# Attention on Trainium2: the products by V issued four key chunks at a time in every fourth unit

## The reference, cut to what matters

```python
n_heads = 16
B, L, D = x.shape
head_dim = D // n_heads
qkv = (x @ Wqkv + bqkv).reshape(B, L, 3, n_heads, head_dim)
q, k, v = (qkv[:, :, 0], qkv[:, :, 1], qkv[:, :, 2])
scores = jnp.einsum('bqhd,bkhd->bhqk', q, k) / math.sqrt(head_dim)
...
scores = scores + slopes[None, :, None, None] * bias[None, None]
probs = jax.nn.softmax(scores, axis=-1)
out = jnp.einsum('bhqk,bkhd->bqhd', probs, v).reshape(B, L, D)
return out @ Wout + bout
```

## Time and profile before

| | us |
|---|---|
| median of 3 runs (3433.7 to 3438.01) | 3435.34 |
| the profiled execution | 3434.41 |
| its span, first to last instruction | 3432.8 |
| TensorE busy (92% of the span) | 3145.6 |
| VectorE busy (68%) | 2335.4 |
| ScalarE busy (53%) | 1823.5 |
| GpSimd busy (31%) | 1072.7 |

### The profile page before, as it was taken

How to read it: one execution, slowest core, us unless ns; L and a number is a source line. 1 busy time by engine, 2 the same in 40 slices (tenths; PEclk the granted TensorE clock), 3 DMA queues, 4 the chain that set the end, 5 groups by cost and what they waited for, 6 DMA issues and landing times. The chain is left out here.

```text
span 3432.8 us, 56926 instructions
## 1 busy us (share of the span) xinstructions
PE 3145.6 (92%) x19234; PEld 2279.5 (66%) x19234; DVE 2335.4 (68%) x4173; ACT 1823.5 (53%) x3126; POOL 1072.7 (31%) x949
## 2 busy tenths in 40 slices
PE   6999899999999999969999699889999999958997
PEld 5777566666666666657777577768888888724443
DVE  5563788888888888845454488875444444599996
ACT  3342788888888888822222322232222222249995
POOL 3343422232222222234433345541100111015666
PEclk9999999999999999989999799999999999989999
DMA  6774322132212221255653634441111011211112
GB/s 213 243 242 173 105 64 60 58 92 63 61 58 85 70 62 58 96 182 184 224 181 113 214 119 137 131 150 50 44 44 32 31 44 31 90 46 50 62 50 74
DMA packets 239350, 350.52 MB, mean 102 GB/s; under 512 B 31792, under 2 KB 129104, under 8 KB 239184
## 3 DMA queue, kind: packets, MB, share of 16 engines
q1 hardware_dynamic: 208256, 290.41, 26.2%
q0 software_dynamic: 8912, 32.82, 2.9%
q10 hardware_dynamic: 22016, 25.17, 2.1%
HBM read 210.68 MB, written 137.64 MB: 101 GB/s over the span
## 5 line engine op out<-in xcount | busy, mean ns | idle before, releaser
L887 DVE CUSTOM_DVE_ANT_0 attend_scores<-attend_scores,attend_bias_table 128x1024 f32<-128x1024 f32 x512 | 630.2, 1231 | 163.9 <-PE attend_scores L741 160.5
L814 ACT ACTIVATE attend_probs<-attend_scores,attend_neg_max 128x1024 f32<-128x1024 f32 x512 | 571.6, 1116 | 140.2 <-DVE attend_neg_max L887 130.6
L753 PE MATMUL attend_turned<-ident,attend_probs 128*128 128x128 f32 x4096 | 556.5, 275 | 12.5 <-DVE attend_probsT L895 12.3
L753 PEld LDWEIGHTS attend_turned<-ident,attend_probs 128*128 128x128 f32 x4096 | 472.0, 140 | 121.1 <-DVE attend_probsT L895 30.3
L741 PE MATMUL attend_scores<-attend_k_stack,attend_q_stack 96*128 96x512 f32 x1024 | 372.6, 445 | 17.6 <-DMA attend_q_stack<-qk_parts 14.5
L822 ACT COPY attend_probsT<-attend_turned 128x512 f32<-128x512 f32 x640 | 359.5, 583 | 24.0 <-PE attend_turned L753 22.5
L2235 DVE TENSOR_TENSOR cross_ffn_h_lo<-cross_ffn_hidden,cross_ffn_h_hi 128x512 fp32r<-128x512 f32 x128 | 104.5, 822 | 340.0 <-ACT cross_ffn_h_hi L2126 339.4
L768 PE MATMUL attend_out_acc<-attend_probsT,attend_v_in 128*32 128x256 f32 x4096 | 312.9, 389 | 0.7 <-DVE attend_out_full L905 0.7
L703 POOL TENSOR_TENSOR attend_out_parts<-attend_out_full,attend_out_parts 128x256 fp32r<-128x256 f32 x64 | 46.6, 728 | 845.8 <-ACT attend_out_parts L829 845.8
L741 PEld LDWEIGHTS attend_scores<-attend_k_stack,attend_q_stack 96*128 96x128 f32 x1024 | 153.9, 189 | 175.0 <-issue 157.5
L895 DVE COPY attend_probsT<-attend_turned 128x512 f32<-128x512 f32 x384 | 263.4, 686 | 1.0 <-PE attend_turned L753 1.0
(11 more groups left out here) (296 smaller groups left out, 6673.6 us busy)
## 6 DMA issues: line engine op xcount, KB each, us to landing
qk_parts<-qkv_qk_out SPq DMA_DIRECT2D x64, 512.0 KB, 3.2
attend_k_stack<-qk_parts SPq DMA_DIRECT2D x192, 128.0 KB, 2.5
attend_q_stack<-qk_parts SPq DMA_DIRECT2D x192, 128.0 KB, 2.7
qkv_wq_raw<-L_ffn_w POOLq DMA_DIRECT2D x16, 1024.0 KB, 7.7
o_parts<-attend_out_parts ACTq DMA_DIRECT2D x64, 256.0 KB, 2.5
carried_o_in<-o_parts SPq DMA_DIRECT2D x32, 512.0 KB, 6.3
qkv_x_in<-x SPq DMA_DIRECT2D x8, 1024.0 KB, 5.7
v_rows<-qkv_v_out SPq DMA_DIRECT2D x32, 256.0 KB, 3.4
```

The costliest lines, as they stand in the source:

```text
L753: last = pe.transpose(turned[:, x, c], probs[:, i % 2, k * P:(k + 1) * P], ident[:, :])
L814: act.activation(probs[:, i % 2], scores[:, i % 2], ACT.Exp, bias=neg_max[:, i % 4:i % 4 + 1], scale=-1.0, accum_out=den[:, qg % 2, j, h:h ...
L887: dve.tensor_tensor_reduce(scores[:, i % 2], scores[:, i % 2], bias_table[:, h, at:at + T], -1.0, BIG, ALU.add, ALU.min, neg_max[:, i % 4: ...
```

## The change

In `before` of TensorE's list the chunks of V are issued only in steps 3 and 7, four at a time: chunks 0 to 3 in step 3, ahead of `turn_den`, and chunks 4 to 7 in step 7. The products themselves, their number and their operands stay as they are, as do the lists of the other engines.

```diff
                     qg, k = i // PER_GROUP, i % PER_GROUP
                     if exists(turn, qg, 1):
-                        if k > 0:
-                            times_v(turn, qg, k - 1)
-                        if k == PER_GROUP - 1:
-                            times_v(turn, qg, k)
+                        if k % 4 == 3:
+                            for c in range(k - 3, k + 1):
+                                times_v(turn, qg, c)
                         if k == 3:
                             turn_den(turn, qg)
```

## The result

The changed kernel takes 3491.54 us (median of 4 runs, 3488.6 to 3493.26) against 3435.99 us: a ratio of 1.0163, 95% interval 1.0149 to 1.0176. The forecast was 3492. The profiled execution took 3491.77 us, its span is 3490.2 us (before 3432.8).

A forecast was written before the change was run, and what follows sets the result against it. The prediction took TensorE to bound the attention loop; after the change a chain through VectorE and then the four-chunk run makes a group 18.24 us instead of 17.34, +0.90 over 63 groups, +57 us: 3492 us, range 3470 to 3516.

The forecast's parts named there:

- (a): Rival: TensorE's saving of five visits comes through, 15.89 us a group, -91 us, 3343 us; chance 0.07.
- the first group, which has no V: Start of the attention loop: four score pairs without V took 1.83 us each, with TensorE waiting for the exponential.
- the empty steps must be paid for: Steps 0 to 2 and 4 to 6: TensorE has 1.36 us of work each, and the other engines can't keep up.
- the 1.89 that two chunks had let expect: Four V chunks in a row on TensorE: 0.57 + 3 x 0.44 = 1.89 us, priced from single and double chunks.
- First half: Score pair 2 to score pair 6 of a group: 9.47 us forecast against 8.51 before the change, +0.96.
- second half: Score pair 6 to the next group's score pair 2: 8.77 us forecast against 8.83 before the change, -0.06.
- the 5.13 us of VectorE: VectorE's work without a hole, from the maximum to unit 2's copy; claimed not to depend on where V stands.
- the two ways of equal length: From score pair 6's maximum to unit 6's copy: VectorE alone 4.65 us, through the score buffer 4.66 us.
- ScalarE's copy of the row sums: Just before unit 6's exponential: if it delays that in full, +0.38 us in each group, +24 us, 3516 us.
- the five visits saved: TensorE's visits to the products by V, seven to two a group: 5 x 0.29 = 1.45 us less work.
- (b): Rival: the two effects cancel, steps without V running at 1.72 us; time would be 3435 us; chance 0.03.
- (c): Rival: TensorE's pauses let the chip lower its clock in the loop, +73 us more, 3565 us; chance 0.04.

The follow-up runs named there:

- 1,2,1,0,1,1,2,0: Chunks of V issued in steps 0 to 7 in these numbers, instead of the unchanged kernel's 0,1,1,1,1,1,1,2; 3379.89 us, ratio 0.9845 to the unchanged kernel.
- 4,0,0,0,4,0,0,0: V chunks by step: four each in steps 0 and 4, instead of the changed kernel's steps 3 and 7; 3437.77 us, ratio 1.0004 to the unchanged kernel.
- 0,4,0,0,0,4,0,0: V chunks by step: four each in steps 1 and 5, instead of the changed kernel's steps 3 and 7; 3479.62 us, ratio 1.0130 to the unchanged kernel.
- 0,0,4,0,0,0,4,0: V chunks by step: four each in steps 2 and 6, instead of the changed kernel's steps 3 and 7; 3490.40 us, ratio 1.0163 to the unchanged kernel.
- 2,0,2,0,2,0,2,0: V chunks by step: two each in steps 0, 2, 4 and 6, instead of the unchanged kernel's 0,1,1,1,1,1,1,2; 3415.65 us, ratio 0.9948 to the unchanged kernel.

## Why the prediction was right

**What bounds the kernel.** Taking TensorE's 99% at face value would have given rival (a), 3343 us. The list of waits and the first group, which has no V, showed that steps without V, one after another, cannot keep to TensorE's 1.36 us each; that the empty steps must be paid for was the step that decided.

**What the change removes.** A run of four chunks holds TensorE 1.87 us against the 1.89 that two chunks had let expect, and the records of V fall from 312.9 to 248.2 us on the page. The page of the changed kernel, transposes and products by V (columns: line, engine, operation, tiles, count | busy us, mean ns of one | idle us before, releaser):

```profile
L753 PE MATMUL attend_turned<-ident,attend_probs 128*128 128x128 f32 x4096 | 599.8, 281 | 51.3 <-DVE attend_probsT L894 49.8
...
L768 PE MATMUL attend_out_acc<-attend_probsT,attend_v_in 128*32 128x256 f32 x4096 | 248.2, 383 | 0.7 <-DVE attend_out_full L904 0.7
```

The same rows show a point I had wrong: I expected TensorE's busy time in the loop to fall. Its share fell, but the sum did not (1080.71 in 1140 us against 1072.73 in 1085). The transposes grew from 556.5 to 599.8 us, and one reason can be seen in the group above: eight transposes that nothing held up (1048.96) are recorded with 1.04 us, the eight at 1054.72, ahead of the lump, with 1.14. I take it that a transpose whose successor waits is recorded as longer; that is not shown for the whole sum. Busy time of TensorE is not a measure of its work; only distances between starts are.

**What it adds.** First half 9.47 walked, 9.45 measured; second half 8.77 walked, 8.75 measured. That the 5.13 us of VectorE stay whole was the term with the most in it, and the trace has them to the hundredth. In the second half the two ways of equal length do end together: the maximum at 1044.05 follows both the copy before it and score pair 8, which started 0.93 us earlier (1043.12). ScalarE's copy of the row sums, for which I kept 0.38 us in the range, cost nothing that can be seen.

**The sum.** 63 groups at 0.90 us gave 57; the stage took 54.2 more, the mean group 0.84 more, so each group was forecast 0.06 us too dear. The span grew by 57.4 all the same, because 3.0 us come from behind the stage, where nothing was changed. Those 3 us are chance: in the profiled executions of the twelve kernels that part takes between 1954.8 and 1961.6 us. That the forecast of 3492 lies within 1 us is therefore luck in part; the mechanism and the two halves are not.

**The rivals.** (a), the saving comes through, fell: the five visits saved were paid for with longer waits. The kernel 1,2,1,0,1,1,2,0 shows that waits weigh more than visits: it saves one visit, 0.29 us, and gains 17.35 - 16.47 = 0.88 us a group. (b) is out, since the group took 18.19 us and not 17.34. (c), a lower clock in the loop, happened once in the changed kernel, for a few us in the last group of the loop (0.50 from 1511 to 1513, in the window above), and was worth some 1.5 us, not the 73 of the rival. The pauses of 0.2 to 0.4 us in every group left the clock at 1.00.

## What to carry to other kernels

When an engine fills its row of the profile, ask of each piece of its work not only how long it is but what the other engines may do beside it: the same two lumps cost nothing in steps 0 and 4 and 56 us in the steps just before, 7 and 3. Write down the distances from one engine's start to the next engine's start, add them along each way through one period, and take the longest; of eleven kernels told in advance, three of them with halves measured in the changed kernel, ten lie within 9 us and one, after a correction that nothing supported, by 13. One of the ten, with the lump in steps 2 and 6, lies there in part by luck: a distance that is taken from one kernel can change in another. A stretch without the disputed work, such as a loop's first round, shows what the others can do alone.

## What the runs showed of the hardware

Unlooked for: VectorE's widened copy of the reciprocals (128x256 in SBUF, 0.29 us in the group of the earlier trace rows and as the median of seven kernels) took 0.81 to 0.85 us (median of 64) in five of them: 4,0,0,0,4,0,0,0, 0,4,0,0,0,4,0,0, 0,0,4,0,0,0,4,0, 2,0,2,0,2,0,2,0 and 1,2,1,0,1,1,2,0. In the last of these it starts while GpSimd subtracts two SBUF tiles; the timelines of GpSimd and of VectorE there:

```profile
1019.63 0.73 POOL L703 TENSOR_TENSOR attend_out_parts<-attend_out_full,attend_out_parts 128x256 fp32r<-128x256 f32 x1 [2.04 <-ACT attend_out_parts L828]
```

```profile
1019.70 0.82 DVE L912 COPY attend_rden_wide<-attend_rden 128x256 f32<-128x256 f32 x1
```

In the kernel with one chunk in each step it starts 0.65 us later than GpSimd's instruction, near its end, and takes 0.29; again GpSimd and VectorE:

```profile
1008.02 0.73 POOL L703 TENSOR_TENSOR attend_out_parts<-attend_out_full,attend_out_parts 128x256 fp32r<-128x256 f32 x1 [16.29 <-ACT attend_out_parts L828]
```

```profile
1008.67 0.29 DVE L912 COPY attend_rden_wide<-attend_rden 128x256 f32<-128x256 f32 x1
```

In the first case both end together but for 0.16 us (1020.36 and 1020.52). The Trainium skill, "SBUF — State Buffer", says in its section Terms, on the shared port pair, that VectorE and GpSimd hold it for a whole instruction and that the loser waits; the first pair of rows agrees in the main; in the second the two overlap by 0.08 us with no delay to be seen, which the rule alone would not give. The five kernels hold a comparison of their own: in the first group with products by V, where GpSimd's instruction does not run yet, the widened copy takes 0.29 us in each of them. A move of chunks on TensorE thus made an instruction of VectorE almost three times as long, by moving what GpSimd does beside it.

What that costs depends on the place. In 4,0,0,0,4,0,0,0 the next maximum starts 1.44 us after the widened copy both in that first group (0.29) and in the later ones (0.85), so it costs nothing. In 0,0,4,0,0,0,4,0, by the rows shown under the experiments, it stands in the chain ahead of the lump with 0.47 us a group. In 2,0,2,0,2,0,2,0 too VectorE has no hole from it to the copy that the transposes ahead of the next pair wait for (0.40 us idle), so that kernel may be held back by it. No run removes it alone.
